# Mixing with checked sums in place of clip and floor and one set of ScalarE tables, and the last output tile made and stored in two halves

## The reference

```python
ek = exp(minimum(k, 30)); ekv = ek * v
nf, df = scan(a * decay + ekv), scan(b * decay + ek)          # forward
nb, db = the same two scans, backward
euk = exp(minimum(u + k, 30))
num = nf + nb - ekv + euk * v
den = df + db - ek + euk
mix = sigmoid(r) * num / maximum(den, 1e-8) * (0.8 + 0.2 * tf)
h = mix @ W1.T
out = x + gelu(0.1 * round(h / 0.1)) @ W2.T
```

## Time and profile before

| what | value |
|---|---|
| time, median of 3 runs | 1795.56 us (1794.16 to 1796.93) |
| the profiled execution's own time | 1794.38 us |
| its span, first to last instruction | 1791.5 us |
| mean granted TensorE clock | 0.985 |
| TensorE busy | 1696.8 us, 95% of the span |
| VectorE busy | 1177.8 us, 66% |
| ScalarE busy | 1071.3 us, 60% |
| DMA, mean | 179 GB/s |
| 0 to 119 us: TensorE, VectorE busy | 38.55, 108.64 us |
| 0 to 119 us: share of the 16 DMA engines | 0.82 |

### The profile page before, as it was taken

How to read it: one execution, slowest core, us unless ns; L and a number is a source line. 1 busy time by engine, 2 the same in 40 slices (tenths; PEclk the granted TensorE clock), 3 DMA queues, 4 the chain that set the end, 5 groups by cost and what they waited for, 6 DMA issues and landing times.

```text
span 1791.5 us, 27197 instructions
## 1 busy us (share of the span) xinstructions
PE 1696.8 (95%) x10882; PEld 1066.3 (60%) x10882; DVE 1177.8 (66%) x1737; ACT 1071.3 (60%) x1471; POOL 24.6 (1%) x44
## 2 busy tenths in 40 slices
PE   1379999999999999999999999999999999999998
PEld 0124444786458854687448864588546874488643
DVE  8977875688666675768765776677867676633211
ACT  5668752787348863598627873489635985245300
POOL 0000020000000000000000000000000000000000
PEclk9779999999999999999999999999999999999999
DMA  9857784755555644665547545556445655455442
GB/s 241 185 148 224 257 300 153 246 179 181 168 174 182 201 135 155 204 206 178 167 126 227 177 164 173 174 183 217 141 156 192 199 166 160 139 174 166 139 133 80
DMA packets 109234, 321.13 MB, mean 179 GB/s; under 512 B 12720, under 2 KB 12720, under 8 KB 108592
## 3 DMA queue, kind: packets, MB, share of 16 engines
q1 hardware_dynamic: 106416, 296.28, 51.2%
q0 software_dynamic: 2688, 23.07, 5.7%
HBM read 310.91 MB, written 48.23 MB: 200 GB/s over the span
## 4 chain that ended last, share of the span: by engine, by line
PE 74%; DMA 3%; DVE 3%; issue 1%; ACT 1%; SPq 0%; DVEq 0%; ACTq 0%
PE ps L519 38%; PE ps L575 36%; DMA x_in<-in_x_dram 2%; DMA chk_full<-in_w_dram 1%; DMA VP<-in_fside_dram 1%; DVE chk_full L1157 1%; ACT L677 0%; DVE y_out L1149 0%; DVE ND L1022 0%; DVE ND L1042 0%; DVE ND L1026 0%; DVE RCP L983 0%; ACT L684 0%; ACT RCP L678 0%; DVE ND L1047 0%
## 5 line engine op out<-in xcount | busy, mean ns | idle before, releaser
L575 PE MATMUL ps<-act,w_ring 128*128 128x512 f16 x4096 | 889.2, 379 | 4.3 <-DVE y_out L1149 4.3
L519 PE MATMUL ps<-mo,w_ring 128*128 128x256 f16 x6272 | 689.6, 273 | 2.8 <-ACT ps L720 2.5
L575 PEld LDWEIGHTS ps<-act,w_ring 128*128 128x128 f16 x4096 | 401.1, 98 | 484.2 <-issue 6.6
L519 PEld LDWEIGHTS ps<-mo,w_ring 128*128 128x128 f16 x6272 | 612.5, 98 | 81.0 <-issue 4.5
L1140 DVE SCALAR_TENSOR_TENSOR act<-a,act 128x1024 f16<-128x1024 f32 x128 | 156.2, 1221 | 159.8 <-ACT act L769 159.8
L1149 DVE SCALAR_TENSOR_TENSOR y_out<-ps,x_in 128x512 f32<-128x512 f32 x64 | 44.1, 690 | 197.2 <-PE ps L575 125.4
L777 ACT ACTIVATE q<-chk_full 128x1024 int8<-128x1024 f32 x64 | 67.0, 1047 | 144.5 <-DMA chk_full<-in_w_dram 144.5
L763 ACT ACTIVATE a<-q 128x1024 f32<-128x1024 int16 x128 | 135.4, 1057 | 15.4 <-DVE act L1140 11.1
L769 ACT ACTIVATE act<-a 128x1024 f16<-128x1024 f32 x128 | 134.2, 1049 | 0.9
L496 PE MATMUL ps<-mo,w_ring 128*128 128x512 f16 x128 | 42.0, 502 | 80.5 <-DVE mo L1075 80.5
L1157 DVE SCALAR_TENSOR_TENSOR chk_full<-q,chk_full 128x1024 f32<-128x1024 int8 x64 | 78.0, 1219 | 57.8 <-ACT q L777 57.8
(11 more groups left out here) (102 smaller groups left out, 1299.1 us busy)
## 6 DMA issues: line engine op xcount, KB each, us to landing
w_ring<-w1s SPq DMA_DIRECT2D x168, 512.0 KB, 3.7
w_ring<-w_half SPq DMA_DIRECT2D x144, 512.0 KB, 4.3
chk_full<-in_w_dram SPq DMA_DIRECT2D x64, 512.0 KB, 4.6
V<-in_fside_dram SPq DMA_DIRECT2D x64, 256.0 KB, 4.6
R<-in_x_dram SPq DMA_DIRECT2D x64, 256.0 KB, 5.0
w_half<-in_w_dram POOLq DMA_DIRECT2D x16, 1024.0 KB, 8.0
x_in<-in_x_dram SPq DMA_DIRECT2D x64, 256.0 KB, 5.6
out_dram<-y_out SPq DMA_DIRECT2D x64, 256.0 KB, 5.0
```

The lines of the kernel that those rows point to most:

```text
L519: mm = pe.matmul(dst[:, f, :], wp_ring[:, k, r, f, q, :], mo[:, op, q, p, :], start=(fresh and f == 0 and q == 0 and p == 0), stop=(q == K ...
L575: mm = pe.matmul(y_ps[y][:, :], w2_ring[:, k, f, :], act[:, a, p, :], start=(a == 0 and p == 0), stop=(a == FT - 1 and p == 1))
```

## The change

The mixing no longer clips the exponentials and no longer applies a floor to the denominator. In their place the sums that ScalarE's instructions accumulate are checked in the vote: the sum of exp(V) as before, the sum of exp(-V) in place of the sum of squares, and a new sum of exp(-R). The gate's tanh becomes exp(-R), and 1 + exp(-R) multiplies the denominator instead of the numerator, so that Exp and Ln from one set of tables do all of the mixing; the reciprocal then waits for the gated denominator. `prefix_argument` leaves the mixing (the general path keeps it): ScalarE makes exp(VP) and the weight exp(ramp * log decay) as two activations, and VectorE multiplies them with a sum. `EK` and `EKV` lie side by side in `EE`, so one instruction adds both bonuses. The last output tile of the last block is made as two products chains of 256 tokens with a result and a store each, and all of the vote but its last step stands ahead of its results.

```diff
             def exps(g, settled):
...
-                sc.preload_act_table_set(EXP_SET)
                 if late:
-                    act_e.wait_ge(s_arg, pg + 1)
-                    sc.activation(EKP[:, :], EKP[:, :], ACT.Exp, accum_out=pre_d[:, c:c + 1]).then_inc(s_ekp, 1)
+                    act_e.wait_ge(s_vp[pg % 2], 16 * (pg // 2 + 1))
+                    if pg > 0:
+                        act_e.wait_ge(s_decayed, pg)
+                    sc.activation(EKP[:, :], VP[:, pg % 2, :], ACT.Exp).then_inc(s_ekp, 1)
...
                 sc.activation(EK[:, k, :], V[:, k, :], ACT.Exp, accum_out=ksum[:, g:g + 1]).then_inc(s_ekx, 1)
+                if late:
+                    act_e.wait_ge(s_ramp, 3)
+                    act_e.wait_ge(s_lndec, B + 1)
+                    sc.activation(EKV[:, k, :], RAMP[:, :], ACT.Exp, scale=lndec[:, b, c:c + 1]).then_inc(s_weight, 1)
...
-                sc.activation(RCP[:, :], V[:, k, :], ACT.Square,
+                sc.activation(RCP[:, :], V[:, k, :], ACT.Exp, scale=-1.0,
                               accum_out=vsum[:, g:g + 1]).then_inc(s_vsq, 1)
...
-                sc.activation(R[:, g % 2, :], R[:, g % 2, :], ACT.Tanh, scale=0.5).then_inc(s_tanh, 1)
+                sc.activation(R[:, g % 2, :], R[:, g % 2, :], ACT.Exp, scale=-1.0,
+                              accum_out=rsum[:, g:g + 1]).then_inc(s_sig, 1)
...
             def weigh(g):
...
-                    v.scalar_tensor_tensor(out=EKV[:, k, :], in0=EKP[:, :], scalar=1.0, in1=VP[:, pg % 2, :],
+                    dve.wait_ge(s_weight, pg + 1)
+                    v.scalar_tensor_tensor(out=EKV[:, k, :], in0=EKP[:, :], scalar=1.0, in1=EKV[:, k, :],
+                                           op0=ALU.mult, op1=ALU.mult, accum_out=pre_d[:, c:c + 1]).then_inc(s_decayed, 1)
+                    dve.wait_ge(s_decayed, pg + 1)
+                    v.scalar_tensor_tensor(out=EKV[:, k, :], in0=EKV[:, k, :], scalar=1.0, in1=VP[:, pg % 2, :],
                                            op0=ALU.mult, op1=ALU.mult, accum_out=pre_n[:, c:c + 1]).then_inc(s_dot, 1)
+                    dve.wait_ge(s_dot, pg + 1)
                 dve.wait_ge(s_ekx, g + 1)
-                v.tensor_scalar(EK[:, k, :], EK[:, k, :], EXP_CLIP, None, ALU.min).then_inc(s_ek, 1)
-                dve.wait_ge(s_ek, g + 1)
...
             def sums(g):
...
-                v.scalar_tensor_tensor(out=DEN[:, k, :], in0=EK[:, k, :], scalar=bonus[:, b, c:c + 1], in1=DEN[:, k, :],
-                                       op0=ALU.mult, op1=ALU.add).then_inc(s_den2, 1)
-                v.scalar_tensor_tensor(out=NUM[:, k, :], in0=EKV[:, k, :], scalar=bonus[:, b, c:c + 1], in1=NUM[:, k, :],
-                                       op0=ALU.mult, op1=ALU.add).then_inc(s_num2, 1)
-                dve.wait_ge(s_den2, g + 1)
-                v.tensor_scalar(DEN[:, k, :], DEN[:, k, :], floor[:, b, c:c + 1], None, ALU.max).then_inc(s_den3, 1)
-                dve.wait_ge(s_num2, g + 1)
-                dve.wait_ge(s_tanh, g + 1)
-                v.scalar_tensor_tensor(out=NUM[:, k, :], in0=R[:, k, :], scalar=1.0, in1=NUM[:, k, :],
+                v.scalar_tensor_tensor(out=ND[:, k, :, :], in0=EE[:, k, :, :], scalar=bonus[:, b, c:c + 1],
+                                       in1=ND[:, k, :, :], op0=ALU.mult, op1=ALU.add).then_inc(s_sums, 1)
+                dve.wait_ge(s_sums, g + 1)
+                dve.wait_ge(s_sig, g + 1)
+                v.scalar_tensor_tensor(out=DEN[:, k, :], in0=R[:, k, :], scalar=1.0, in1=DEN[:, k, :],
                                        op0=ALU.add, op1=ALU.mult).then_inc(s_gate, 1)
...
+            def output_end(n, d):
+
+                slots = [loaded(), loaded()]
+                pe.wait_ge(s_res[1], DT // 2 * n + d // 2)
+                for c in range(2):
+                    for a in range(FT):
+                        for p in range(2):
+                            mm = pe.matmul(y_end[c], w2_ring[:, slots[a // (FT // 2)], a % (FT // 2), :],
+                                           act[:, a, p, c * H:(c + 1) * H],
+                                           start=(a == 0 and p == 0), stop=(a == FT - 1 and p == 1))
+                    mm.then_inc(s_yend if c == 0 else s_y, 1)
```

More of the change, by code:

```diff
@@ L132, in adaln_ffn_kernel @@
         bonus = sb("bonus", [P, B, CT], F32)
-        floor = sb("floor", [P, B, CT], F32)
+        gap = sb("gap", [P, B, CT], F32)
         eu_sb = sb("eu_sb", [P, CT], F32)
@@ L423, in _ @@
             store(BLOCKS - 1, DT - 2)
-            store(BLOCKS - 1, DT - 1)
+            store_end(BLOCKS - 1, DT - 1)
             for k in range(2):
-                sp.wait_ge(s_store[k], 16 * (DT // 2) * BLOCKS)
+                sp.wait_ge(s_store[k], 16 * (DT // 2 * BLOCKS + k))
             def general_block(m):
@@ L598, in _ @@
                 output(n, 1, 1)
-                for d in range(2, DT):
+                for d in range(2, DT if n + 1 < BLOCKS else LAST):
                     output(n, d, 0)
                     output(n, d, 1)
-            pe.wait_ge(s_vote, 12)
-            pe.matmul(f_ps[0:1, 0:1], verdict[:, 9:10], ones[:, :], start=True, stop=True).then_inc(s_votes, 1)
+            output_end(BLOCKS - 1, LAST)
+            pe.wait_ge(s_vote, 13)
+            pe.matmul(f_ps[0:1, 0:1], verdict[:, 0:1], ones[:, :], start=True, stop=True).then_inc(s_votes, 1)
             def general_block(m):
@@ L1147, in result, with result_end @@
                 if uses > 0:
-                    dve.wait_ge(s_store[k], 16 * uses)
+                    dve.wait_ge(s_store[k], 16 * (uses + (k if n >= BLOCKS else 0)))
                 v.scalar_tensor_tensor(out=y_out[:, k, :], in0=y_ps[k][:, :], scalar=scale, in1=x_in[:, k, :],
                                        op0=ALU.mult, op1=ALU.add).then_inc(s_res[k], 1)
+            def result_end(n, d):
+                uses, last = DT // 2 * n + d // 2, y_half(n, d, 0)
+                dve.wait_ge(s_x[1], 16 * (uses + 1))
+                dve.wait_ge(s_store[1], 16 * uses)
+                dve.wait_ge(s_yend, 1)
+                v.scalar_tensor_tensor(out=y_out[:, 1, 0:H], in0=y_end[0], scalar=1.0 / ACT_SCALE, in1=x_in[:, 1, 0:H],
+                                       op0=ALU.mult, op1=ALU.add).then_inc(s_resend, 1)
+                dve.wait_ge(s_y, last)
+                v.scalar_tensor_tensor(out=y_out[:, 1, H:T], in0=y_end[1], scalar=1.0 / ACT_SCALE, in1=x_in[:, 1, H:T],
+                                       op0=ALU.mult, op1=ALU.add).then_inc(s_res[1], 1)
             def residual_sum(n, d):
```

161 lines of the change are left out of this document (88 added, 73 removed).

## The result

The median is 1775.39 us (1774.23 to 1776.02, 4 runs) where the kernel before took 1796.12 us (1794.16 to 1796.93, 4 runs): a ratio of 0.9885 (95% interval 0.9868 to 0.9903), 20.7 us faster. The direction was right and so were most of the mechanisms. The size was short: 14.6 us were forecast and 20.7 measured. The step that failed is the price of the seed's waits at the block ends, put at 1.3 us where they cost 4.27.

A forecast was written before the change was run, and what follows sets the result against it. TensorE was taken as the bound, with time to gain only at the start (set by VectorE), in waits, and at the end. Savings of 8.5 + 4.5 + 1.3 + 0.3 = 14.6 us gave 1781.0 us, range 1776.8 to 1786.5.

The forecast's parts named there:

- the seed's waits at the block ends: TensorE's four waits for ScalarE's seed copy (L720), 2.5 us idle: an earlier chain should free most, 1.3 us (0.3 to 2.3).
- The start: TensorE's 80.5 us idle before its first product: a tile period of 12.0 instead of 13.19 us, saving 8.5 us (6.8 to 10).
- the first weighing: VectorE's first weighing, begun at 10.20 us before: put 1.5 us sooner, with fewer table loads and VectorE instructions ahead.
- stall at the third tile: At the start, VectorE would wait 1.1 us for ScalarE's copy L695, queued behind the late load of VP.
- each instruction of VectorE counts: At the start VectorE has only 0.21 us idle per 13.19 us tile, so its time was taken as the bound.
- the separate 0.29 us: Between gate and L1075, VectorE's wait for ScalarE's L695 in each start tile: 0.29 us counted as its own saving.
- Block 0: TensorE's 4.3 us wait for result L1149: 3.1 us saved plus 1.4 us of low clock behind it, 4.5 us (1.2 to 5.7).
- The rival in which the landing holds L707: In block 0, L707 still waits for the weight-sum store, so that block gives only 1.2 us: 1784.3 us, chance 0.20.
- The end: Last output tile and final flag: shorter result and half-size store give 0.3 us (0 to 0.8), SyncE being held by the store.
- The rest hidden behind TensorE: More than 120 table loads, 64 clips and 64 floors on ScalarE and VectorE, hidden behind TensorE: worth nothing.
- To the median: From the profiled execution's like, 1779.8 us, to the median forecast, 1781.0 us: 1.2 us added.
- more than forecast: Rival: no third-tile stall, all of block 0's 4.3 and 1.4 us, both seed waits gone: 17.8 us, 1777.8 us, chance 0.13.

The follow-up runs named there:

- Experiment 3: Kernel before without VectorE's clip and floor: 1790.82 us; then the same with ScalarE's copy of the mixed tile ahead of the next tile's exponentials: 1787.21 us.
- experiment 2: Kernel before with one table load per tile group instead of three: 1786.90 us; changed kernel with two loads per group put back from the second eight tiles: 1786.91 us.
- experiment 1's second: Kernel before with only the halved last output tile, its two results and stores and the votes ahead of them, mixing unchanged: 1794.39 us (ratio 0.9992).
- e2, e3, e6, e10, e11: One of five edits of the kernel before that keep the gate's Tanh, measured at 1787.21 to 1797.33 us; the text does not say which.

## Why the prediction was right in kind and short in size

- **The start (8.5; 8.18).** Close in each term that the rows show: period 11.93 for 12.0, the first weighing 1.30 us sooner (10.20 to 8.90) for 1.5, one stall at the third tile of 0.96 us for 1.1, the last group of products at 104.77 (113.72 less 8.95). The 32 products then took 9.52 us instead of 8.75, more of them at the low level; I had named up to 1.7 us either way for it. One sentence was wrong: that at the start each instruction of VectorE counts. Experiment 3 shows that the loop through ScalarE set the period, that the separate 0.29 us was its visible end, and that the floor taken away by itself gives nothing. (ScalarE has eight instructions in a tile, not about nine.)
- **Block 0 (4.5; 4.95).** The wait fell to 0.67 us instead of 1.1, and there was no slow stretch behind it: 83.04 us for 384 products, where it was 84.39. The rival in which the landing holds L707 did not come: ScalarE's copy still waited for that landing (3.05 us, 3.42 in the earlier trace rows), but it began at 217.30 where it had been 230.82, and the landing was not what held the result. Behind that copy ScalarE waited for VectorE's sums in both kernels (1.26 us before, 3.01 after).
- **L720's waits (1.3; 4.27): the step that failed.** I took the idle rows (2.5 us in all, 2.1 in the two long waits) as the price and put the gain at 1.3. Two errors are in it. The idle column holds only part of the cost: in the rows of before the 32 products from 321.46 to 326.16 take 4.70 us from start to start, where the same 32 take 3.49 elsewhere (422.38 to 425.87), so 1.21, and the next group has 89.47 for 89.24; together 1.44 us for a row that says 1.04. The last of the six periods holds 1.66 us for a row that says 1.09. The four ends that I took for free had 0.23 to 0.36 us each, two of them with no idle row at all (92.97 for 92.74 at 739.90). And "should free most" had to be "all": experiment 2 shows that taking away the table loads brings all six periods to 208.32. At the end of block 0 the chain needed only to come 1.2 us earlier, and it came 1.6 earlier: the seed stands 2.40 us behind the block's start now, it was 3.98.

```profile
309.77 1.06 ACT L814 ACTIVATE q<-chk_full 128x1024 int8<-128x1024 f32 x1 [2.09 <-DMA chk_full<-in_w_dram]
310.73 0.58 ACT L757 ACTIVATE ps<-ps 128x512 f32<-128x512 f32 x1
```

- **The end (0.3; 0.90 in this pair, 1.3 over all traces).** I took the store's landing for what holds the span's end. In the rows, from the last result's start to its store's issue it is 0.45 us where it was 0.72, the second store lands 1.7 us after its issue in place of 2.1, and from that landing to the end of the span it is 4.1 us in place of 4.5. So the shorter result gave what I had for it, and the rest comes from the store of half the bytes and from behind the landing; what part the votes have in it was not told apart.
- **The rest hidden behind TensorE (0)** was right for the kernel as changed, and experiment 2 shows how near the edge: with two loads a group put back, waits appear inside blocks.
- **To the median.** I kept the 1.2 us between the profiled execution and the median for both kernels; after, the profiled execution lies 0.1 above its median. The waits that the change removes may be part of what makes the kernel before vary: its six periods hold 4.27 us in one execution and 5.67 in another kernel with the same mixing (experiment 1's second), while after they hold none. That this is the cause is not shown. With 2.97 us more for the block ends and 0.6 to 1.0 for the end, the sum would have been about 18.5 and the forecast 1777; the range was too short on that side, as its "more than forecast" case kept the seed's waits at 2.1.

## What to carry to other kernels

Price a wait by the distance between the starts of the same work with and without it, not by the idle column: for pipelined products part of a stall is written down as busy time. Where several short waits hang on one chain, ask by how much the chain must come earlier for all of them to go; beyond that they go together, and before that moving the late instruction on one engine can only move the wait to the next. Sum such waits over more than one execution: here one trace was good to 1.5 us. An instruction saved on the pacing engine counts only if no loop through the other engine is longer: look for the small idle time that another engine ends, and follow it round once.

## What was not expected of the hardware

- Idle time of about 3.2 us ahead of the same 384 products was followed by slow ones in two kernels (84.73 us, after 3.13 and 3.27 us, with a granted clock of 0.50 for some 3 us) and by none in a third (83.04 us, after 3.32 us, granted clock 1.00). After 1.75 us and less none was slow; after 4.0 to 4.5 us, in four kernels, it was 84.39 to 85.92.
- 24 products of zeros, put right behind the sixth tile's at the start, kept the upper level: the 16 real ones behind them took 3.63 us, 227 ns each, at a granted clock of 1.00.
- The time outside the span was 1.8 to 1.9 us in all runs of the two kernels that begin with a memset on GpSimd, and 2.2 to 2.4 in the changed kernel; since the span begins with the first recorded instruction, this may be only where it is cut. In the kernel before it was 2.2 to 4.9 in 46 runs. It reached 3.5 us and more in each of the five experiments that keep the gate's Tanh (e2, e3, e6, e10, e11), and stayed at 2.2 to 2.4 in all 26 runs of kernels whose gate is an Exp and that have no memset, the one with its table loads put back too. Why is open.
